# Decoder layer on one core: where four bias additions run, how many units are folded, and how the first projections are dealt out

## The reference, cut to what matters

```
# x, ctx: (32, 128, 128) f32; 16 heads of 8
x1  = layernorm(x  + self_attention(x) @ wo.T + bo)          # q, k, v with biases bq, bk, bv
x2  = layernorm(x1 + cross_attention(q=x1, k=ctx, v=ctx) @ Wo.T)
h   = gelu(qlinear(x2, W1, b1))                              # 128 -> 512
out = layernorm(x2 + qlinear(h, W2, b2))                     # 512 -> 128
# qlinear: one scale and zero point for the whole tensor, from its minimum and maximum;
# the integers of x and of W are multiplied, and the product is scaled back
```

## Time and profile before

| what | us |
|---|---|
| runs, median | 332.87 |
| runs, lowest and highest | 332.35, 334.61 |
| profiled execution | 331.59 |
| its span | 329.9 |
| DVE busy | 299.9 (91% of the span) |
| PE, ACT, POOL busy | 269.5, 248.1, 238.6 |

### The profile page before, as it was taken

The page is one execution under the profiler, slowest core; times in us unless marked ns, Lnnn a source line. Parts: engine busy times, 40 slices in busy tenths (PEclk is TensorE's granted clock), DMA queues, the critical chain, the costliest instruction groups (busy, mean ns, idle before and its releaser), DMA issues.

```text
span 329.9 us, 12489 instructions
## 1 busy us (share of the span) xinstructions
PE 269.5 (82%) x4927; PEld 168.4 (51%) x4927; DVE 299.9 (91%) x695; ACT 248.1 (75%) x502; POOL 238.6 (72%) x477
## 2 busy tenths in 40 slices
PE   4677987999999999999999988898887655536991
PEld 3455654666656566665656655555554212112561
DVE  5668799899999999999999999999988779987994
ACT  2237776989988888888888878788775399912995
POOL 2866787897677878687786887776559228998394
PEclk9999999999999999999999999999999897557797
DMA  2353324143342423334243234322100000000025
GB/s 65 111 152 92 108 76 129 52 125 92 107 122 64 123 67 115 84 99 125 69 123 92 79 97 131 90 78 61 52 5 0 3 0 0 1 0 0 2 79 177
DMA packets 48993, 25.14 MB, mean 76 GB/s; under 512 B 6440, under 2 KB 48808, under 8 KB 48936
## 3 DMA queue, kind: packets, MB, share of 16 engines
q1 hardware_dynamic: 46072, 23.55, 24.6%
q10 hardware_dynamic: 2864, 0.80, 1.0%
HBM read 9.39 MB, written 2.10 MB: 35 GB/s over the span
## 4 chain that ended last, share of the span: by engine, by line
POOL 36%; DVE 29%; issue 13%; PE 10%; ACT 5%; SPq 3%; DMA 2%; POOLq 1%; DVEq 0%; ACTq 0%
DVE neg_max L1044 15%; POOL rstd L640 5%; SPq L472 3%; POOL arena_h L670 3%; POOL var_eps L633 2%; ACT arena_h L903 2%; DMA arena_h<-parts_sk 2%; POOL parts_cq L439 2%; POOL parts_ck L439 2%; PE ps L1298 2%; POOL parts_cq L437 2%; POOL parts_ck L437 2%; POOL x_bias L659 2%; DVE o_stats L1206 1%; POOL parts_sq L439 1%
## 5 line engine op out<-in xcount | busy, mean ns | idle before, releaser
L1044 DVE TENSOR_REDUCE neg_max<-ps 128x8 f32<-128x1024 f32 x128 | 156.2, 1220 | 9.5 <-PE ps L1298 9.3
L852 ACT ACTIVATE probs<-ps 128x1024 f32<-128x1024 f32 x64 | 65.5, 1024 | 21.8 <-PE ps L1305 21.8
L843 ACT ACTIVATE probs<-ps 128x1024 f32<-128x1024 f32 x64 | 65.6, 1025 | 15.7 <-PE ps L1305 11.8
L1298 PE MATMUL ps<-arena_h 31*128 31x128 f16 x1024 | 52.3, 220 | 20.4 <-DVE neg_max L1044 11.2
L1298 PEld LDWEIGHTS ps<-arena_h 31*128 31x128 f16 x1024 | 30.5, 94 | 54.9 <-DVE neg_max L1044 38.4
L1305 PE MATMUL ps<-arena_h 32*128 32x128 f16 x1024 | 51.2, 217 | 0.9 <-ACT probs L852 0.9
L1326 PE MATMUL ps<-probs,arena_q 128*32 128x128 f32 x1024 | 41.2, 279 | 1.4 <-ACT u_sb L868 1.4
L1326 PE MATMUL ps<-probs,arena_h 128*32 128x128 f32 x1024 | 41.3, 279 | 0.0
L633 POOL TENSOR_TENSOR var_eps<-mean_var,eps_col 128x1 f32<-128x1 f32 x64 | 12.3, 192 | 38.1 <-DVE mean_var L1026 38.1
L640 POOL TENSOR_TENSOR rstd<-var_eps,minus_half 128x1 f32<-128x1 f32 x64 | 35.3, 551 | 4.7
L1305 PEld LDWEIGHTS ps<-arena_h 32*128 32x128 f16 x1024 | 29.2, 92 | 2.0 <-ACT probs L852 1.5
(11 more groups left out here) (182 smaller groups left out, 657.7 us busy)
## 6 DMA issues: line engine op xcount, KB each, us to landing
arena_h<-parts_sq SPq DMA_DIRECT2D x48, 64.0 KB, 1.9
arena_h<-parts_ck SPq DMA_DIRECT2D x48, 64.0 KB, 2.3
arena_h<-parts_sk SPq DMA_DIRECT2D x46, 64.0 KB, 2.0
arena_h<-parts_cq SPq DMA_DIRECT2D x45, 64.0 KB, 2.2
xT_in<-in_xT_dram SPq DMA_DIRECT2D x16, 128.0 KB, 2.5
xN_in<-in_xN_dram SPq DMA_DIRECT2D x16, 128.0 KB, 2.6
cT_in<-in_cT_dram SPq DMA_DIRECT2D x16, 128.0 KB, 2.5
cN_in<-in_cN_dram SPq DMA_DIRECT2D x16, 128.0 KB, 2.3
```

The lines of the kernel that those rows point to most:

```text
L843: act.activation(probs[1][:, :], ps_s2, ACT.Exp, scale=SCALE).then_inc(ex, 1)
L852: act.activation(probs[0][:, :], ps_s2, ACT.Exp, scale=SCALE).then_inc(ex, 1)
L1044: dve.tensor_reduce(neg_max[b.par][:, HH * half:HH * half + HH], ps_s1.rearrange("p (h k) -> p h k", h=HH), AXX, ALU.max, negate=True).the ...
L1298: ins = pe.matmul(ps_s1[:, at:at + S], q[r:r + MAX_AT, j, :], kk[r:r + MAX_AT, j, :], start=True, stop=True, skip_group_check=True)
```

## The change

- **Biases.** The four `x2_bias` run on POOL directly behind the slots, ahead of the first integers of x, instead of between the folds. They no longer write in place but into `arena_x`, a new tile in which `x_bias` and the split terms `parts` lie until then. The fourth waits until the last x2 is written; the first three wait for nothing. The residual matmuls read `arena_x`.
- **Folds.** Five units are folded (3, 6, 9, 11, 13) instead of four, and DVE's order follows.
- **Ramp.** From slot -2 to slot 2 one projection (q, k or v of a pair) stands behind each burst, from the table `RAMP`, where before q and k stood together behind both bursts of a slot. To part the sums, k of pairs 0 to 2 goes to `ps_u`, v of pairs 1 and 2 to banks 2 and 3, which the shifted scores use later; two waits guard that. q's projection releases its evacuation alone instead of together with k's. ACT evacuates them one at a time.
- **What moves with it.** `setup_products` goes behind slot 0's second burst; `blocks()` on POOL from slot -2 to slot 0; POOL splits q and k of pair 3 in slots 0 and 1 instead of 1 and 2. `xT_in` has four buffers; the loads of pairs 2 and 3 are issued at the very start.

Core of the diff (left out: the semaphores' count, the bodies of `v_out`, `project_q`, `project_k` and `project_v`, which hold what stood in `evacuations` and `projections`, each projection now with an increment of its own):

```
-LOADS = 2
+LOADS, X_LOADS = 2, 4
...
-LEAD_SLOTS = 2
+
+RAMP = {(-2, 0): ("v", 1), (-2, 1): ("q", 2), (-1, 0): ("k", 2), (-1, 1): ("v", 2), (0, 0): ("q", 3),
+        (1, 0): ("k", 3), (1, 1): ("v", 3), (2, 0): ("q", 4), (2, 1): ("k", 4)}
+RAMP_FIRST, RAMP_LAST = -2, 2
...
-FOLDED_UNITS = (3, 6, 9, 12)
-EXTREMES_ORDER = (1, 2, 4, 5, 3, 7, 8, 6, 10, 11, 9, 13, 14, 12, 15)
+FOLDED_UNITS = (3, 6, 9, 11, 13)
+EXTREMES_ORDER = (1, 2, 4, 5, 3, 7, 8, 6, 10, 12, 9, 14, 11, 15, 13)
...
+        arena_x = sb("arena_x", [128, B * D])
+        x_bias = [arena_x[:, i * 2 * D:(i + 1) * 2 * D].rearrange("p (i d) -> p i d", i=2) for i in range(RING)]
         q_full, k_full, ck_full = sb("q_full", [128, PAIR]), sb("k_full", [128, PAIR]), sb("ck_full", [128, PAIR])
         cq_full = [sb(f"cq_full{i}", [128, PAIR]) for i in range(RING)]
-        parts = {n: [sb(f"parts_{n}{i}", [128, 2, PAIR], F16) for i in range(PARTS)] for n in NAMES}
+        parts_words = arena_x[:, 2 * D * RING:]
+        parts = {n: [parts_words[:, (PARTS * j + i) * PAIR:(PARTS * j + i + 1) * PAIR].bitcast(F16)
+                     .rearrange("p (s t) -> p s t", s=2) for i in range(PARTS)] for j, n in enumerate(NAMES)}
...
+        def q_sums(i):
+            return ps_p[:, 0:PAIR]
+
         def k_sums(i):
 
-            return ps_u[:, 0:PAIR] if i == 0 else ps_p[:, PAIR:2 * PAIR]
+            return ps_u[:, 0:PAIR] if i < 3 else ps_p[:, PAIR:2 * PAIR]
+
+        def v_sums(i):
+
+            return bank(1 + i)[:, 0:2 * D] if i in (1, 2) else ps_p[:, 0:2 * D]
...
-                if i >= LOADS:
-
-                    sp.wait_ge(pvv, i - LOADS + 1)
-                sp.dma_start(xT_in[i % LOADS][:, :], xT[:, i * PAIR:(i + 1) * PAIR]).then_inc(s_xT[i % LOADS], 16)
+                if i >= X_LOADS:
+
+                    sp.wait_ge(pvv, i - X_LOADS + 1)
+                sp.dma_start(xT_in[i % X_LOADS][:, :], xT[:, i * PAIR:(i + 1) * PAIR]).then_inc(s_xT[i % X_LOADS], 16)
...
             sp.dma_start(wv_sb[:, :], wv).then_inc(w_v, 16)
+            load_xT(2)
+            load_xT(3)
...
                 i = S_FIRST.get(k + FILL_AT)
-                if i:
+                if i and i != 3:
                     pool.wait_ge(eqk, 2 * i + 2)
                     split(pool, "sk", k_full[:, :], i)
...
-                i = S_FIRST.get(k + QK_AT)
-                if i:
+                i = 3 if k == 0 else S_FIRST.get(k + QK_AT)
+                if i and not (i == 3 and k != 0):
+
+                    if i == 3:
+                        blocks()
                     pool.wait_ge(eqk, 2 * i + 1)
                     split(pool, "sq", q_full[:, :], i)
...
                 if k == -2:
                     pool.memset(arena_h[:, (RING + 2) * words:2 * RING * words], MROW_PAIR)
                     pool.memset(arena_h[:, 2 * words:RING * words], 0.0).then_inc(rest_cleared, 1)
-                    blocks()
+                if k == 1:
+
+                    pool.wait_ge(eqk, 2 * 3 + 2)
+                    split(pool, "sk", k_full[:, :], 3)
...
             def x2_bias(c):
-                t = x2_all[:, c * 8:(c + 1) * 8, :]
-                pool.tensor_tensor(t, t, b2_wide[:, :].unsqueeze(1).broadcast_to([128, 8, D]),
-                                   ALU.add).then_inc(f_b, 1)
+
+                if c == B // 8 - 1:
+                    pool.wait_ge(xn, made_to(C_POS[B - 1], False))
+                pool.tensor_tensor(arena_x[:, c * 8 * D:(c + 1) * 8 * D].rearrange("p (b d) -> p b d", d=D),
+                                   x2_all[:, c * 8:(c + 1) * 8, :],
+                                   b2_wide[:, :].unsqueeze(1).broadcast_to([128, 8, D]), ALU.add).then_inc(f_b, 1)
...
@@ -731,19 +756,14 @@
                 fold(h[:, 0:CH // 2], h[:, CH // 2:], probs[0][:, 0:CH // 2], probs[0][:, CH // 2:],
                      *[y_out[2 * (n % 2) + m][:, :, :].rearrange("p b d -> p (b d)") for m in range(2)], f_fold)
 
+            for c in range(B // 8):
+                x2_bias(c)
             x_ints(2)
             x_ints(3)
             fold_unit(0)
             x_ints(4)
-            fold_unit(1)
-            pool.wait_ge(f_xi, DVE_PIECES)
-            pool.wait_ge(f_xp, NP - DVE_PIECES)
-            x2_bias(0)
-            fold_unit(2)
-            x2_bias(1)
-            fold_unit(3)
-            x2_bias(2)
-            x2_bias(3)
+            for n in range(1, len(FOLDED_UNITS)):
+                fold_unit(n)
...
+                def q_out(i):
+                    if i == 0:
+                        act.wait_ge(b_ready, 1)
+
+                    act.wait_ge(pqk, 2 * i + 2 if i == LEAD_PAIRS - 1 else 2 * i + 1)
+                    need(act, split_done["sq"], i)
+                    act.activation(q_full[:, :], q_sums(i), ACT.Identity, bias=bqk_sb[:, 0:1]).then_inc(eqk, 1)
+
+                def k_out(i):
+                    act.wait_ge(pqk, 2 * i + 2)
+                    need(act, split_done["sk"], i)
+                    act.activation(k_full[:, :], k_sums(i), ACT.Identity, bias=bqk_sb[:, 1:2]).then_inc(eqk, 1)
...
-                if k >= LEAD_SLOTS:
+                if RAMP_FIRST < k <= RAMP_LAST:
+                    ramp_out(k, 0)
+                elif k == RAMP_LAST + 1:
+                    ramp_out(RAMP_LAST, 1)
+                elif k > RAMP_LAST:
                     evacuations()
                 if a is not None:
                     act.wait_ge(p2, 2 * a.pos + 1)
@@ -860,8 +901,12 @@
                     for t, part in enumerate(Q_PARTS):
                         act.dma_start(stack["cq"][0][t::ROW_STEP, :, :],
                                       parts["cq"][0][:, part, :]).then_inc(stacks_landed("cq", 0)[0], 16)
-                if k < LEAD_SLOTS:
+                if k < RAMP_FIRST:
                     evacuations()
+                elif k == RAMP_FIRST:
+                    ramp_out(k, 0)
+                if k < RAMP_LAST:
+                    ramp_out(k, 1)
...
                     if s is not None:
+                        if s.pos == 0 and s_half == 0:
+
+                            pe.wait_ge(evv, 3)
...
                     if half == 0:
+                        if z.pos == 0:
+
+                            pe.wait_ge(eqk, 2 * 2 + 2)
...
+                def ramp(half):
+
+                    name, i = RAMP.get((k, half), (None, None))
+                    if name == "q":
+
+                        if i < 4:
+                            pe.wait_ge(eqk, 2 * i - 1)
+                        else:
+                            pe.wait_ge(evv, i)
+                        project_q(i)
+                    if name == "k":
+
+                        pe.wait_ge(eqk, 2 * i if i < 3 else 2 * i + 1)
+                        project_k(i)
+                    if name == "v":
+                        if i > 2:
+                            pe.wait_ge(eqk, 2 * i + 2)
+                        project_v(i)
...
-                if k == 0:
-
-                    setup_products()
...
-                if k == LEAD_SLOTS:
-                    projections(k)
+                ramp(0)
                 scores(1)
                 product(1)
-                if k < LEAD_SLOTS:
+                if k < RAMP_FIRST:
                     projections(k)
+                if k == 0:
+
+                    setup_products()
+                if k < RAMP_LAST:
+                    ramp(1)
...
-                if k >= LEAD_SLOTS:
+                if k == RAMP_LAST:
+                    ramp(1)
+                if k > RAMP_LAST:
                     projections(k + 1)
...
             def residual(g):
                 pe.wait_ge(f_b, g // 2 + 1)
-                pe.matmul(bank(g), ident_out[:, :], x2_all[:, 4 * g:4 * g + 4, :].rearrange("p b d -> p (b d)"),
+                pe.matmul(bank(g), ident_out[:, :], arena_x[:, 4 * g * D:(4 * g + 4) * D],
```

More of the change, by code:

```diff
@@ L192, in xT_pairs @@
 def xT_pairs(k):
-    ahead = [(i, XT_AT if i < LEAD_PAIRS else XT_LATER_AT) for i in range(LOADS, PAIRS)]
+    ahead = [(i, XT_AT if i < LEAD_PAIRS else XT_LATER_AT) for i in range(X_LOADS, PAIRS)]
     return [i for i, at in ahead if S_POS[2 * i] - at == k]
@@ L250, in decoder_layer @@
         arena_q = sb("arena_q", [128, NHC * B * S // 2])
-        xT_in = [sb(f"xT_in{i}", [128, PAIR]) for i in range(LOADS)]
+        xT_in = [sb(f"xT_in{i}", [128, PAIR]) for i in range(X_LOADS)]
         cT_in = [sb(f"cT_in{i}", [128, PAIR]) for i in range(LOADS)]
@@ L330, in decoder_layer @@
         w_out, w_cross, w_ffn = sem("w_out_landed"), sem("w_cross_landed"), sem("w_ffn_landed")
-        s_xT = [sem(f"xT_landed{i}") for i in range(LOADS)]
+        s_xT = [sem(f"xT_landed{i}") for i in range(X_LOADS)]
         s_cT = [sem(f"cT_landed{i}") for i in range(LOADS)]
@@ L825, in evacuations @@
[L825 to L832 removed]
+                        v_out(i)
@@ L1330, in product, with project_q, project_k, project_v @@
                     last.then_inc(pv, 1)
+                def project_q(i):
+                    if i == 0:
```

(21 more changed lines are left out.)

70 lines of the change are left out of this document (27 added, 43 removed).

## The result

| | before | after |
|---|---|---|
| runs side by side on one chip, median us (lowest to highest) | 333.02 (332.05 to 334.61) | 334.38 (333.13 to 336.10) |
| ratio after / before, 95% interval | | 1.004 (1.0024 to 1.0057) |
| profiled execution; its span | 331.59; 329.9 | 334.33; 332.6 |
| DVE, PE, ACT, POOL busy | 299.9, 269.5, 248.1, 238.6 | 302.5, 274.1, 248.6, 242.0 |

The change makes the kernel 0.4% slower: more than the interval, and less than the 1% that I had set as the bound of no change. The forecast was 333.1 in a range of 329.5 to 335.7. The forecast time came from case A, the measured one is that of rival B (334.3), and the profile shows B's mechanism too.

What follows compares the result with a forecast made beforehand. Bound by a chain of waits through POOL and DVE, with DVE full mid-kernel, so only the ends count: start -1.6, folds -2.3, moved biases +4.1, sum +0.2 on median 332.87 gives 333.1 us; range 329.5 to 335.7.

Steps and rivals of the forecast that it cites:

- case A: The chosen forecast: biases hold DVE's new x2 and integer pieces, small steps stay free; total +0.2, 333.1 us; chance 0.42.
- rival B: Behind the last root, small steps reading two SBUF columns wait for biases too; +5.3, total +1.4, 334.3 us; chance 0.25.
- Folds, -2.3: Feed forward stage: without biases between folds, POOL's last fold ends at 297.1, last extreme at 298.4 for 300.78; -2.3 us.
- Moved biases, +4.1: Last root to integers: POOL's biases delay the new x2 by 2.0, then the integer pieces; +4.1 us altogether.
- the zero for the small steps: DVE's 128x1 and 2x2 steps between new x2 and integers: not held by biases, 0 each (bounds 0 and 2.3).
- The start, -1.6: Pipeline start to slot 3: sum of the ramp's gains and losses, -1.6 us, bounds -0.9 and -2.2.
- (a): Slot 0: first burst goes earlier with only v of pair 2 ahead, maximum at 20.4, 0.6 us earlier.
- (c): Slot 2: pair 2's projections move earlier, its landing is no longer last; slot 2 starts at 28.4, 1.2 us earlier.
- (d): Slot 3: one matmul instead of q and k stands in front of the burst; 0.4 us more gained.
- (b): Slot 1: q of pair 3 and setup products take up the gain; maximum of 26.22 at 26.0, only 0.2 earlier.
- The rest follows DVE's pace: Behind the start: DVE is full mid-kernel, so a shift won at the start is carried to its end.
- The waits added on TensorE, the row of maxima and the early loads: Pipeline start: two extra TensorE waits, ACT's row of maxima 1.3 us later, two early xT loads; costed at nothing.

Runs made afterwards that it cites:

- `tail_only`: Kernel before with only the new tail: `arena_x`, biases directly behind the slots, five folds; 335.78 us, ratio to before 1.0065.
- `spread`: Kernel after with biases off DVE's chain: one behind DVE's integers, one between POOL's integers, two behind the last fold; 332.23 us, ratio to before 0.9953.
- `ramp_only`: Kernel after's new start with the kernel before's tail: four folded units, biases between folds; 332.15 us, ratio to before 0.9942.
- `gated`: Kernel after with the first bias waiting until DVE has written the last x2; 334.23 us, ratio to before 1.0022.
- `one_input`: Kernel after with the two steps of two SBUF columns rewritten as one tensor and a scalar pointer; 333.67 us, ratio to before 1.0033.
- `short_pieces`: Kernel after with each bias split into four POOL instructions of 128x256; 330.56 us, ratio to before 0.9933.
- `spread_four`: `spread` with four folded units (3, 6, 9, 12) instead of five; 330.22 us, ratio to before 0.9913.
- `memsets_wait`: `cq_behind_2` with POOL's memsets of slots 5 and 11 waiting until DVE has written that slot's new x; 328.96 us, ratio to before 0.9907.
- `cq_behind_2`: Repeat run of `spread_four` with ACT's three cq DMAs issued behind slot 8's copy of u instead of ahead; 329.50 us, ratio to before 0.9914.

## Why the prediction was right, and where it was not

The sum was +0.2, made of -1.6 -2.3 +4.1. The runs give:

- **Folds, -2.3.** Right. -2.38 in the profile, as worked out: POOL is last, a fold each 4.50 us, the last fold's end 1.32 us ahead of the last extreme's (predicted 1.3). `tail_only` has the same 32.78.
- **Moved biases, +4.1.** The mechanism was right and the term too small: +5.06. The step that failed is the zero for the small steps ("no row shows one stopped; bounds are 0 and 2.3 each. I take 0 for them"). The new x2 lost 2.00 (predicted 2.0). Then 0.25 went to the 2x2 step, 0.3 to TensorE between (its answers took 0.46 and 0.68 of waiting for 0.36 and 0.49), 1.07 to the first step of two columns and 1.53 to the second, together 5.15, and the integers, for which I had put down 2.1, lost nothing (0.73 for 0.83). This is rival B to 0.2 us: it had the first such step wait to 265.05 (265.23), the next to 267.4 (267.53), and both pieces done at 268.7 (268.67), though it did not have the 2x2 step held. B had a chance of 0.25; A, with the small steps free, 0.42.
- **Why I chose A.** The nearest row, 301.68 with 0.22, stood at the very end of a bias, and I said so, but still counted it as evidence. `spread` shows that the same step is held (2.30). A row in which two operations only touch at their ends tells nothing of what happens when they overlap.
- **The rule behind it.** The rule of the Trainium skill ("SBUF — State Buffer", section "Who interferes with whom") that a VectorE operation with two SBUF inputs contends with a GpSimd operation that reads SBUF, is borne out by 1.23 and 1.68 for 0.16 and 0.15, and by 0.21 and 0.20 once the second input is a pointer to scalars. The Trainium skill ("DVE: scalar operands, raw-bit mode, write accounting and state across instructions", section "1. Scalar operands") says that such a pointer does not take up the second tensor stream; the trace agrees (0.21 and 0.20).
- **The start, -1.6.** By the time of `ramp_only` about right as a sum, 1.9 faster (1.0 to 2.8), but in part by luck: the forecast had its 1.6 in place at slot 3, where the profile has 1.0. (a) Slot 0 came 0.58 earlier, predicted 0.6. (c) Pair 2's landing left the chain, as predicted. (d) At slot 3 the pipeline led by 1.0, and at slot 9 by 1.7. (b) was wrong: the maximum of 26.22 came at 26.88, where I had 26.0, and slot 2 at 29.21, where I had 28.4. The chain shows the reason: the three setup products, 16 products with v and k of pair 3, all of them on TensorE, one behind the other from 22.34 on. The setup products alone took 1.58, where I had about 1. In `gated`, `one_input` and `short_pieces`, whose start is the same code, slot 2 came at 28.5 to 28.7, near the forecast. What differs is TensorE's pace (below).
- **Then most of the lead was lost**, in two places which I had not looked at. Between slots 9 and 10 the kernel after gives back 1.5 of its 1.7 us; `spread` and `spread_four` do so too, the others with the new start 0.3 at most, and the difference is the clock (below). Between slots 10 and 13, 0.5 to 0.8 us go in the kernel after and in most of the others, in the step that POOL's memsets hold; `memsets_wait` shows it. That is not the new start's doing, since `tail_only` loses 0.8 there too: the profile of before had a short case of it. "The rest follows DVE's pace" was the phrase that hid both: a lead is carried on only as far as the next place whose length varies by itself. The profile of `ramp_only` has its last root only 0.2 ahead of that of before and a span 0.2 shorter, while its time is 1.9 better. The two profiled executions were not equally good ones: 331.59 is 1.4 under the median of the kernel before in its own row of runs (1.8 under the 333.42 of the later one), 331.47 only 0.7 under that of `ramp_only`. So the size of the start's gain rests on the times, and the profiles show where it arises and goes.
- **The rest.** The waits added on TensorE, the row of maxima and the early loads were costed at nothing, and the chain does not show them.

Terms of -1.6, -2.3 and +4.1 (5.1 in truth) nearly cancel, so the total came out within half a per cent of nothing with either price of the port; the total alone would not have told A from B, the durations of the four DVE steps did. That the total came out in the range says little for the port's term.

## What to carry to other kernels

Idle time of POOL next to a chain of short DVE steps is not free room: what runs there holds DVE to the end of the instruction that is running, so a chain of small steps is caught by one long instruction after another until they are all done. Such filler belongs where DVE does reductions (the chain takes 5.28 for 10.37 us in `spread_four`, which is 1.3% faster as a whole), or in short instructions (7.04). Freeing one step of such a chain brings nearly nothing as long as a later one is caught (0.2 of 2.0 us).

## What the runs showed of the hardware that I had not expected

**A DVE step of 2x2 is held as long as one of 128x512; its form decides.** Held until a POOL addition ended: 128x128 (2.35 for 0.35), 2x2 (2.30 for 0.22), 128x512 (2.54 for the pair, 0.73 free), all tensor_scalar from SBUF to SBUF; two columns of 128x1 as two tensors (1.68 for 0.15). Not held under the same additions: tensor_scalar on one column of 128x1 (0.15 to 0.22), reductions, and steps that read PSUM. Why a column passes and a 2x2 doesn't was not tried. The Trainium skill ("VectorE: DVE Perf Modes", section "Mode 2×_2P — use both read ports for one tensor") says that this mode splits one tensor in two halves along its outermost non-unit dimension, which has to be even, or odd and equal for source and result. A column of one element has no such dimension, which would fit; no run here shows it.

**Between short memsets in a row DVE is let in at no fixed place.** Behind POOL's biases of 2.3 us DVE was let in at the next end each time. Among memsets the same step with the same five instructions took 1.36, 1.71, 1.83, 2.12 or 2.46 us in one profile or another: the end of the second, of the third (1.83) or of the last. Where it took 1.71 or 2.46, it had begun while POOL still ran the operation in front of the memsets (a split's, of 0.67 us, in `cq_behind_2` from 66.14 on), and was not let in at that one's end either.

**TensorE ran at about half its pace at the start while the granted clock read 1.00.** The projection of k of pair 3 and the 16 products with v ahead of it, timeline of TensorE of the kernel after:

```profile
24.40 1.08 PE L1377 MATMUL ps<-probs,arena_q 128*32 128x128 f32 x16
25.59 0.92 PE L1394 MATMUL ps<-xT_in,wk_g 128*128 128x256 f32 x2
```

and of `gated`:

```profile
24.45 0.92 PE L1377 MATMUL ps<-probs,arena_q 128*32 128x128 f32 x16
25.41 0.60 PE L1394 MATMUL ps<-xT_in,wk_g 128*128 128x256 f32 x2
```

The granted clock of both in that stretch (columns: stretch, its us, busy us of PE, PEld, DVE, ACT, POOL with counts, granted clock, DMA share, GB/s), the kernel after first:

```profile
24.00:26.00 2.00, 2.00 (x34) 1.32 (x27) 1.49 (x3) 1.19 (x2) 0.00 (x0) 1.00 0.58 163
...
24.00:26.00 2.00, 2.00 (x39) 1.22 (x43) 1.44 (x3) 1.28 (x2) 0.00 (x0) 1.00 0.18 47
```

Matmuls reach their full pace at about 26.5 us in the kernel after and 25.3 in `gated`, whose code is the same up to there. The kernel before had it from 22 us on. This is what slot 2's 28.7 against 29.2 comes from. The later 16 products of the kernel after take 0.57 (26.84, in the chain of waits). What sets the moment is open.

**The granted clock fell in some executions and not in others.** Windows of the kernel after behind the 1.66 us wait of slot 8 (columns as above):

```profile
56.00:58.00 2.00, 1.46 (x20) 1.16 (x21) 0.15 (x1) 1.89 (x6) 1.92 (x5) 0.74 0.27 76
58.00:60.00 2.00, 2.00 (x36) 1.06 (x34) 1.51 (x4) 1.18 (x2) 1.19 (x2) 0.50 0.06 19
```

and of `ramp_only`, which has the same wait (1.67 us):

```profile
56.00:58.00 2.00, 1.42 (x31) 1.02 (x34) 0.27 (x2) 1.91 (x6) 1.92 (x5) 1.00 0.23 66
58.00:60.00 2.00, 2.00 (x54) 1.43 (x46) 2.00 (x7) 1.81 (x5) 1.17 (x2) 1.00 0.06 14
```

At 0.50 (1.2 for 2.4 GHz) TensorE does 36 matmuls in 2 us instead of 54, and slot 10 starts 1.3 us later (61.39 for 60.11). The same idle time has both outcomes, so it alone is not the cause. Of the seven profiles with the new start and this wait, it fell in three (the kernel after, `spread`, `spread_four`) and stayed in four. The wait is not new either: the kernel before (1.40) and `tail_only` (1.64) have it, and in both the clock stayed at 1.00.
